# Three half units of every later attention team: exponentials on VectorE instead of ScalarE

## The reference, cut to what matters

```
q, k, v = (x @ w.T).reshape(B, S, 16, 16).transpose(0, 2, 1, 3)   # for w_q, w_k, w_v, x normalised
scores = einsum("bhqd,bhkd->bhqk", q, k) / sqrt(16)
scores = where(mask == 0, -inf, scores)     # causal, and full among the first 196 tokens
ctx = einsum("bhqk,bhkd->bhqd", softmax(scores), v)
x = x + layernorm(ctx @ w_o.T + b_o)
...                                          # top-2 of 8 experts and a shared one, SwiGLU
x = x + layernorm(ffn(layernorm(x)))
```

## Time and profile before

| | |
|---|---|
| runs | 2376.24, 2378.51, 2379.26 us; median 2378.51 us |
| profiled execution | 2377.52 us; its span, first to last instruction, 2375.8 us |
| mean granted TensorE clock over the span | 0.949 of full speed |
| busy in the span | PE 2127.9 us (90%), ACT 1776.9 (75%), DVE 1303.1 (55%), POOL 700.5 (29%) |
| exponentials, L959 | 1152 instructions, from 217 to 1254 us of the span |

### The profile page before, as it was taken

One profiled execution on the slowest core, in us unless ns is written; L12 is line 12 of the kernel. 1 busy time (PEld: TensorE's weight loads), 2 busy tenths in 40 slices (PEclk: granted clock), 3 DMA queues, 4 the chain that ended last, 5 costly groups with the idle time before them and its releaser, 6 DMA issues. The chain is left out here.

```text
span 2375.8 us, 37728 instructions
## 1 busy us (share of the span) xinstructions
PE 2127.9 (90%) x14197; PEld 1307.5 (55%) x14197; DVE 1303.1 (55%) x2070; ACT 1776.9 (75%) x2250; POOL 700.5 (29%) x700
## 2 busy tenths in 40 slices
PE   5995999999999999999995984999999999999920
PEld 4773333333333333333334873888888888888820
DVE  4663222222222222222224966988888888888848
ACT  4664999999999999999993762555566666666624
POOL 1111000000000000000001533887166666666631
PEclk9997999999999999999997976999999999999965
DMA  6886644555555544444503864888566767777558
GB/s 194 297 304 171 117 87 87 100 100 100 100 98 99 72 83 86 89 86 61 71 10 113 267 193 164 294 288 290 196 165 171 171 171 170 171 171 177 127 135 316
DMA packets 204264, 365.79 MB, mean 154 GB/s; under 512 B 18680, under 2 KB 141176, under 8 KB 195256
## 3 DMA queue, kind: packets, MB, share of 16 engines
q1 hardware_dynamic: 161084, 299.38, 46.9%
q0 software_dynamic: 34256, 55.20, 12.4%
q10 hardware_dynamic: 8748, 8.85, 1.2%
HBM read 219.81 MB, written 143.42 MB: 153 GB/s over the span
## 5 line engine op out<-in xcount | busy, mean ns | idle before, releaser
L959 ACT ACTIVATE att_prob<-att_scores 128x1024 f32<-128x1024 f32 (+2 forms) x1152 | 1022.6, 1047 | 38.2 <-PE att_scores L910 31.0
L929 PE MATMUL att_out<-att_prob,att_va 128*32 128x512 f32 (+3 forms) x5120 | 591.0, 543 | 14.7 <-DVE att_prob L991 14.7
L910 PEld LDWEIGHTS att_scores<-att_qs,att_ks 50*128 50x128 f32 x2560 | 213.1, 185 | 500.9 <-ACT att_prob L959 427.6
L910 PE MATMUL att_scores<-att_qs,att_ks 50*128 50x512 f32 (+3 forms) x2560 | 469.8, 433 | 18.3 <-DMA att_qs<-guard 17.0
L991 DVE SCALAR_TENSOR_TENSOR att_prob<-att_prob,att_tri 128x512 f32<-128x512 f32 x224 | 144.8, 688 | 613.4 <-ACT att_prob L959 613.4
L1485 POOL DMA_INDIRECT sums<-moe_y,moe_token x156 | 346.3, 2220 | 224.7 <-ACT moe_y L1641 189.1
L1548 PE MATMUL moe_ps<-moe_xt_hi,moe_w_hi 128*128 128x512 f32 x880 | 347.4, 395 | 0.0
L1548 PE MATMUL moe_ps<-moe_xt_hi,moe_w_lo 128*128 128x512 f32 x880 | 347.0, 394 | 0.0
L1548 PE MATMUL moe_ps<-moe_xt_lo,moe_w_hi 128*128 128x512 f32 x880 | 345.3, 392 | 0.0
L862 POOL DMA_DIRECT2D ctx_scr<-att_cout x64 | 48.3, 755 | 994.6 <-DVE att_cout L1009 954.1
L929 PEld LDWEIGHTS att_out<-att_prob,att_va 128*32 128x32 f32 x5120 | 111.3, 108 | 189.4 <-issue 96.3
(11 more groups left out here) (193 smaller groups left out, 3041.8 us busy)
## 6 DMA issues: line engine op xcount, KB each, us to landing
moe_wraw<-w_experts SPq DMA_DIRECT2D x55, 1412.0 KB, 6.6
qk_parts<-proj_qk SPq DMA_DIRECT2D x64, 512.0 KB, 4.2
att_qs<-qk_parts SPq DMA_DIRECT2D x180, 128.0 KB
att_ks<-qk_parts SPq DMA_DIRECT2D x180, 128.0 KB
rows_in<-att_zeros SPq DMA_DIRECT2D x13, 1548.0 KB, 21.0
moe_xin<-rows_in SPq DMA_DIRECT2D x39, 516.0 KB, 4.3
proj_xin<-x SPq DMA_DIRECT2D x16, 512.0 KB, 3.9
v_scr<-proj_va SPq DMA_DIRECT2D x16, 512.0 KB, 3.5
```

The costliest lines, as they stand in the source:

```text
L910: last = nc.tensor.matmul(pss[e % SBUFS][:, h, at:at + CH - q0], ks[s][rows, half, kt * P:(kt + 1) * P], qs[s][rows, half, c * CH + q0:(c ...
L929: last = nc.tensor.matmul(pso[k % 2][strip, q0:], va[team % 2][:, kt, strip], prob[u % PBUFS][:, h, at:at + CH - q0], start=(kt == 0), sto ...
L959: nc.scalar.activation(prob[u % PBUFS][:, half * 2:half * 2 + 2, start:], pss[e % SBUFS][:, :, start:], ACT.Exp, scale=HD ** -0.5)\
```

## The change

In teams 1 to 15, units 22 and 23 (chunk 3, key blocks 1 and 2) leave the ring of `prob` tiles and get tiles of their own, `late_prob`. Unit 22 is scored right behind unit 1, and both its halves get their exponentials on DVE. Unit 23 is scored behind unit 24; 23a stays on ACT, and 23b goes to DVE. The values of both are multiplied right behind those of unit 33. On DVE a half takes ten instructions of 128x1024 (`power_of`): stage 0 reads the PSUM tile, scales and bounds it and releases the tile; stages 1 to 3 make the power of two and the fraction, stages 4 to 8 the polynomial, stage 9 the product. One stage is issued per loop turn, at the end of the turn, behind `finish`, `copy`, `cross` and `place`: for 22a at units 1, 3, ... 19, for 22b at units 2, 4, ... 20, for 23b at units 24 to 33. The distances of values, copy, turn and finish are counted in units of the ring now, 34 per team.

```diff
+LATE = {UNITS.index((BCH - 1, ((1, 0, 0),), 0)): (1, (0, 1)), UNITS.index((BCH - 1, ((2, 0, 0),), 0)): (24, (1,))}
+LATE_USED = NU - 3
...
+RING_UNITS = [team * NU + i for team in range(ALL_TEAMS) for i in range(NU) if i not in late(team)]
+for u in RING_UNITS:
+    team, i = divmod(u, NU)
+    LATE_BEHIND[u] = [team * NU + m for m, (behind, _) in late(team).items() if behind == i]
+    SCORE_ORDER += [u] + LATE_BEHIND[u]
+    VALUE_ORDER += [u] + ([team * NU + m for m in late(team)] if i == LATE_USED else [])
...
+        def wait_scores_read(eng, e):
+            if e >= 0:
+                if HALF_ORDER[e] in EXPED_AT:
+                    eng.wait_ge(exped, EXPED_AT[HALF_ORDER[e]])
+                else:
+                    eng.wait_ge(late_read, VECTOR_AT[HALF_ORDER[e]] + 1)
...
-                for u in range(ALL_UNITS + TURN):
-                    if u < ALL_UNITS:
-                        scores(u)
-                    if u - TURN in end_of:
-                        turn(end_of[u - TURN])
-                    if 0 <= u - VALUES < ALL_UNITS:
-                        values(u - VALUES)
+                for r in range(len(RING_UNITS) + TURN):
+                    if r < len(RING_UNITS):
+                        scores(RING_UNITS[r])
+                        for u in LATE_BEHIND[RING_UNITS[r]]:
+                            scores(u)
+                    if r >= TURN and RING_UNITS[r - TURN] in end_of:
+                        turn(end_of[RING_UNITS[r - TURN]])
+                    if 0 <= r - VALUES < len(RING_UNITS):
+                        u = RING_UNITS[r - VALUES]
+                        values(u)
+                        if u % NU == LATE_USED:
+                            for m in late(u // NU):
+                                values(u // NU * NU + m)
...
+                def power_of(u, half, side, stage):
+                    f, p, to = frac[side], poly[side], probs_of(u)[:, half * 2:half * 2 + 2]
+                    step, before = late_step[side], steps_done[side]
+                    if before and stage:
+                        dve.wait_ge(step, before)
+                    if stage == 0:
+                        e = HALF_AT[u, half]
+                        dve.wait_ge(scored, e + 1)
...
+                        wait_probs_free(dve, u)
+                        V.tensor_scalar(f[:], pss[e % SBUFS][:], HD ** -0.5 * LOG2E, LOWEST, ALU.mult, ALU.max)\
+                            .then_inc(late_read, 1)
+                        return
+                    if stage == 1:
+                        dve.wait_ge(late_read, VECTOR_AT[u, half] + 1)
+                        done = V.tensor_scalar(p[:], f[:], ROUND, None, ALU.add)
+                    elif stage == 2:
+                        done = V.tensor_scalar(to.bitcast(I32), p[:].bitcast(I32), 23, None, ALU.logical_shift_left)
+                    elif stage == 3:
+                        done = V.scalar_tensor_tensor(f[:], p[:], ROUND, f[:], ALU.subtract, ALU.subtract)
+                    elif stage == 4:
+                        done = V.tensor_scalar(p[:], f[:], POWERS[-1], None, ALU.mult)
+                    elif stage < POLY - 1:
+                        done = V.scalar_tensor_tensor(p[:], p[:], POWERS[8 - stage], f[:], ALU.add, ALU.mult)
+                    else:
+                        V.scalar_tensor_tensor(to, p[:], 1.0, to, ALU.add, ALU.mult).then_inc(late_done, 1)
+                        return
...
                         if i == PLACE and team + 1 < ALL_TEAMS:
                             place(team + 1, slice(0, BCH))
+                        for m, (behind, halves) in late(team).items():
+                            if behind <= i < behind + POLY * len(halves):
+                                stage, side = divmod(i - behind, len(halves))
+                                power_of(team * NU + m, halves[side], side, stage)
```

More of the change, by code:

```diff
@@ L721, with late @@
 ALL_TEAMS = B * TEAMS
-ALL_UNITS = ALL_TEAMS * NU
+LATE = {UNITS.index((BCH - 1, ((1, 0, 0),), 0)): (1, (0, 1)), UNITS.index((BCH - 1, ((2, 0, 0),), 0)): (24, (1,))}
+LATE_USED = NU - 3
+def late(team):
+    return LATE if team else {}
+RING_UNITS = [team * NU + i for team in range(ALL_TEAMS) for i in range(NU) if i not in late(team)]
+RING_OF = {u: r for r, u in enumerate(RING_UNITS)}
+SCORE_ORDER, VALUE_ORDER, LATE_BEHIND = [], [], {}
+for u in RING_UNITS:
[3 more added lines that the diff above has]
+    VALUE_ORDER += [u] + ([team * NU + m for m in late(team)] if i == LATE_USED else [])
+USED_AT = {u: at + 1 for at, u in enumerate(VALUE_ORDER)}
+HALF_ORDER = [(u, half) for u in SCORE_ORDER for half in range(HALVES)]
+HALF_AT = {uh: e for e, uh in enumerate(HALF_ORDER)}
+BY_VECTOR = [(u, half) for u, half in HALF_ORDER if u not in RING_OF and half in LATE[u % NU][1]]
+BY_SCALAR = [uh for uh in HALF_ORDER if uh not in BY_VECTOR]
+EXPED_AT = {uh: at + 1 for at, uh in enumerate(BY_SCALAR)}
+VECTOR_AT = {uh: at for at, uh in enumerate(BY_VECTOR)}
+LOG2E = 1.4426950408889634
+LOWEST = -126.0
+ROUND = 1.5 * 2.0 ** 23 + 127.0
+POWERS = (-0.6931469775972935, 0.2402224208411893, -0.055507337459397184, 0.009671512697276688, -0.001326472638887228)
+POLY = 10
 def attend(nc, ident, norms, qk_parts, v_scr, guard, ctx_ch, rows_in, sums):
@@ L791, in attend @@
         prob = [ph.sb(f"prob{i}", [P, TEAM, CH]) for i in range(PBUFS)]
+        late_prob = [ph.sb(f"late_prob{i}", [P, TEAM, CH]) for i in range(len(LATE))]
+        frac = ph.sb2("frac", [P, 2, CH])
+        poly = ph.sb2("poly", [P, 2, CH])
         osb = ph.sb2("osb", [P, CH])
@@ L828, in masked_to, with probs_of, wait_probs_free, wait_probs_ready @@
             return u // NU * masked_by[-1] + masked_by[u % NU]
+        late_place = {m: i for i, m in enumerate(LATE)}
+        def probs_of(u):
+            if u in RING_OF:
+                return prob[RING_OF[u] % PBUFS]
+            return late_prob[late_place[u % NU]]
+        def wait_probs_free(eng, u):
+            if u in RING_OF:
+                if RING_OF[u] >= PBUFS:
+                    eng.wait_ge(used, USED_AT[RING_UNITS[RING_OF[u] - PBUFS]])
+            elif u - NU in USED_AT and u - NU not in RING_OF:
+                eng.wait_ge(used, USED_AT[u - NU])
+        def wait_probs_ready(eng, u):
+            for half in range(HALVES):
+                if (u, half) in EXPED_AT:
+                    eng.wait_ge(exped, EXPED_AT[u, half])
+                else:
+                    eng.wait_ge(late_done, VECTOR_AT[u, half] + 1)
+        def wait_scores_read(eng, e):
[4 more added lines that the diff above has]
+                    eng.wait_ge(late_read, VECTOR_AT[HALF_ORDER[e]] + 1)
         def load_guard(eng, team):
@@ L951, in _ @@
                 load_guard(act, 0)
-                for u in range(ALL_UNITS):
-                    wait_from_one(act, used, u - PBUFS + 1)
+                for u in SCORE_ORDER:
+                    wait_probs_free(act, u)
                     start = UNITS[u % NU][2]
                     for half in range(HALVES):
[L957 to L961, removed]
+                        if (u, half) in EXPED_AT:
+                            e = HALF_AT[u, half]
+                            act.wait_ge(scored, e + 1)
+                            nc.scalar.activation(probs_of(u)[:, half * 2:half * 2 + 2, start:],
+                                                 pss[e % SBUFS][:, :, start:], ACT.Exp, scale=HD ** -0.5)\
+                                .then_inc(exped, 1)
             @block.vector
@@ L994, in copy @@
                 def copy(u, k):
-                    dve.wait_ge(used, u + 1)
+                    dve.wait_ge(used, USED_AT[u])
                     wait_from_one(dve, o_turned, k - 1)
                     V.tensor_copy(osb[k % 2][:], pso[k % 2][:]).then_inc(o_copied, 1)
+                def power_of(u, half, side, stage):
[4 more added lines that the diff above has]
+                    if stage == 0:
+                        e = HALF_AT[u, half]
+                        dve.wait_ge(scored, e + 1)
+                        if VECTOR_AT[u, LATE[u % NU][1][0]]:
+                            dve.wait_ge(late_done, VECTOR_AT[u, LATE[u % NU][1][0]])
+                        wait_probs_free(dve, u)
[13 more added lines that the diff above has]
+                        done = V.scalar_tensor_tensor(p[:], p[:], POWERS[8 - stage], f[:], ALU.add, ALU.mult)
+                    else:
+                        V.scalar_tensor_tensor(to, p[:], 1.0, to, ALU.add, ALU.mult).then_inc(late_done, 1)
+                        return
+                    done.then_inc(step, 1)
+                    steps_done[side] += 1
                 def finish(k):
@@ L1022, in _ @@
                 V.tensor_scalar(zeros[:, :, D], zeros[:, :, D], float(T), None, ALU.add).then_inc(z_made, 1)
[L1023 to L1028, removed]
+                steps_done = [0, 0]
+                for r in range(len(RING_UNITS) + FINISH):
+                    if r >= FINISH and RING_UNITS[r - FINISH] in end_of:
```

(5 more changed lines are left out.)

12 lines of the change are left out of this document (6 added, 6 removed).

## The result

The changed kernel takes 2507.15 us (2502.01 to 2509.64, 4 runs) against 2377.38 us in the runs beside it: a ratio of 1.0547, 95% interval 1.0521 to 1.0573, 130 us slower. Forecast were 2495 us, 2445 to 2525.

A forecast was written before the change was run, and what follows sets the result against it. ACT was taken to set the pace in attend. Per team, 8.25 + 0.8 + 0.8 - 2.71 = 7.1 us, plus 0.7 for PE's clock, 7.8; 15 teams add 117 us: 2495 us, range 2445 to 2525.

The forecast's parts named there:

- What bounds it: In attend, ACT sets the pace at 1.81 us a unit, PE needs 1.66; the score queue is three tiles deep.
- The walk: Team's start, 34a to next team's 3'a (prime: next team): 17.2 us in place of 8.94, costing 8.25 a team.
- The hand-over on DVE: At a team's start, successor starts 0.08 us before wide mask's recorded end; by the skill's rule 0.24 us longer a team.
- Unit 24: Behind 25b, scores of 26a come 0.9 us late, less 0.1 standing there before: 0.8 us a team (0 to 1.1).
- Diagonals: At units 7 to 10, DVE stages between masks delay unit 9's copy, 0.7; unit 19's masks 0.1: 0.8 us (0 to 1.2).
- The clock: PE's idling at a team's start halves its clock for 3.41 us: 0 to 1.7 us a team, 0.7 taken.
- my case for 2510 us: The granted clock falls at every team's start, giving 2510 us in place of 2495.
- The sum: 7.1 us a team plus 0.7 for PE's clock makes 7.8; 15 teams, 117 us; forecast 2495 us.
- The signs: Profile after: period near 72.5 us, ACT busy 61, DVE near 48, two waits for stage 0 a team, clock under 1.00.
- ACT's relief is all that is seen: Rival: tiles decouple the engines in attend, so only the 41 us taken off ACT count: 2337 us; chance 0.05.
- only the late values cost: Rival: DVE reads 22a and 22b in time, leaving 0.1 us a team: 2380 us, no change; chance 0.04.
- DVE becomes the bound: Rival: DVE instructions take twice their rows, 80 us a team, 18 more than ACT's 62: 2650 us; chance 0.03.

The follow-up runs named there:

- fill_idle: Changed kernel plus 17 extra matmuls a team (9 and 8) in PE's two idle times at a team's start: 2480.29 us, ratio 1.0431.
- order_only: Changed kernel's new order of units, but all exponentials back on ACT: 2426.63 us, ratio 1.0205.
- reads_first: Changed kernel with stage 0 of 22a and 22b at the top of DVE's turn, ahead of copy and mask: 2440.90 us, ratio 1.0266.
- ballast_quiet: Kernel before plus thirty DVE instructions a team on scratch tiles, at turns of units 10 to 17, 21, 22, 25 to 33: 2378.48 us, ratio 1.0003.
- ballast_only: Kernel before, old order, plus thirty DVE instructions a team on scratch tiles at the turns of the change's stages: 2416.04 us, ratio 1.0168.
- quiet_two: Against the kernel before: only half a of units 22 and 23 on DVE, scored behind units 3 and 15, values behind 26 and 31: 2374.78 us, ratio 0.9987.

## Why the prediction was right

*What bounds it.* ACT with 1.81 us a unit, and a lead of three tiles: held. What is left on ACT is 2.71 us a team less, all of it real.

*The walk.* Against the timeline above, from 34a: 0'a 4.89 (5.22 forecast), 2'a 9.37 (9.6), first stage 0 10.68 (10.97), 2'b 12.44 (12.9), second stage 0 15.39 (15.3), 3'a 17.26 (17.2). Two errors cancel. The late values take 0.86 us each, not 1.0: PE goes from the values of 33 to the next scores in 429.26 - 426.55 = 2.71 us, of which the first take 1.0. And the transposes ran at the low clock, which the walk did not have: 438.35 - 437.31 = 1.04 us, 0.59 before. In the teams of fill_idle without a low stretch, 34a to 3'a is 16.8 us, so at full clock the walk is 0.4 too long. The hand-over on DVE is as in the rows: stage 0 starts 1.14 us after the wide mask, 0.07 ahead of its recorded end. By the sentence of the Trainium skill that the prediction takes from VectorE: DVE Perf Modes (The DRAIN you can't avoid) it would start behind it. The same paragraph adds that an instruction that is not held starts earlier, and with that the records agree.

*Unit 24.* 0.98 us behind 25b in every team. 0.9 was walked, less 0.1 that was to stand there before; but before there is nothing behind 25b, so the term is 0.98 against 0.8. With 23b on ACT (order_only, at full clock) the same place costs 0.08: the exponential taken off ACT here is lost whole.

*Diagonals.* 0.3 us at 12b and 0.1 at 10b; 0.8 forecast, half of it too much.

*The clock.* This term was mis-sized. I took 0.7 us a team, for a low stretch of 3.41 us that falls on work or into idle time. The fall did come at every team's start, which was my case for 2510 us. For a stretch of 3.41 us the 0.7 is right: such teams take some 71.9 us, and 71.2 take those of fill_idle that have none. What I had not thought of is that the clock stays low for 10.24 or 13.65 us in seven of the fifteen teams, which costs 2.9 and 4.4 us against the same 71.2. On average it is 73.34 - 71.24 = 2.1 us a team; fill_idle, in which five teams still have a low stretch, gets 27 us back, 1.8 a team. The 71.24 us are those of a kernel with 17 matmuls more a team; whether these cost anything by themselves, no run shows.

*The sum.* Without the clock 7.1 us a team were forecast, and 71.24 - 64.70 = 6.5 are measured: walk 0.4 and diagonals 0.4 too much, unit 24 0.2 too little. With the clock's 2.1 it is 8.6, 130 us in 15 teams, where I had 7.8 and 117. So the mechanism held, and the number is near because the terms without the clock were too large and the clock's too small; that they offset each other is luck. The range was added up wrongly: its upper bounds together make 8.25 + 0.8 + 1.1 + 1.2 + 1.7 - 2.71 = 10.3 us a team, 2533 us, where 9.6 and 2525 stand (9.5 without the semaphore hops), and its lower end needs unit 24 free as well. The result lies in it either way.

*The signs.* The period near 72.5 us is 73.34, DVE's 48 us a team are 46, ACT's 61 are 61.4, and there are two waits for stage 0 at a team's start, with a third wait of PE's weight loads a team that I had not named. ACT's idle times were to be 2.5 to 3.5 us: behind 2a it is 2.53, behind 2b 4.25, where the low clock adds to the wait (3.7 in fill_idle's teams at full clock).

*The rivals.* That ACT's relief is all that is seen is out: of the late values the tiles' lead hides next to nothing (2 x 0.86 = 1.72 us of work, and 2.12 - 0.46 = 1.66 more standstill behind 35b). That only the late values cost is out by the 2.53 and 4.25 us behind 2a and 2b; with stage 0 ahead of copy and mask, the first is gone and 66 us with it (reads_first). That DVE becomes the bound is out in the form given (ballast_quiet, 1.0003). Its weaker form, that the load costs where it delays masks and copies, I had only at the copy of unit 9; it is worth 39 us in the old order (ballast_only). In the changed kernel it is not paid on top: where the clock is soon back, ACT stands 0.13 us behind 5b and not at all behind 4b, as before.

## What to carry to other kernels

Before work is moved to an idle engine, ask at which place in that engine's program order it will stand, what it will be waiting for there, and what the engines ahead hold until it has run: thirty instructions cost 39 us at one set of turns and nothing at another. Where two engines are level, relief for one is worth only what the buffers between them can carry; in quiet_two each half unit moved gave 0.9 us and took nearly all of it back, and in the change itself the three cost far more than they gave. A change that makes TensorE wait in short pieces can pay a second time in its clock (some 2 of 8.6 us a team here), so look at the granted clock by stretch, not only at the mean.

## What was not expected of the hardware

The clock also falls where PE has no long gap. In order_only it is 0.50 from 469.30 to 472.70, after 3.42 us in which PE was busy for 2.39, with gaps of 0.68 and 0.34 us (windows: length, PE, PEld, DVE, ACT, POOL, clock):

```profile
465.88:469.30 3.42, 2.39 (x20) 0.92 (x18) 0.83 (x2) 3.27 (x5) 0.00 (x0) 1.00 0.00 0
469.30:472.70 3.40, 3.40 (x14) 1.00 (x14) 1.14 (x3) 2.56 (x3) 0.65 (x1) 0.50 0.02 5
```

While it is low, eight matmuls of the values take 1.94 us (438.35 in the kernel after) where the row ahead of the change has 1.06. And once low it can stay so for 13.65 us with PE busy for 12.30 of them (the last window of the kernel after). What decides whether it stays low for 3.41, 10.24 or 13.65 us, no run here settles. Extra matmuls in idle time, which change no result, made the changed kernel 27 us faster.
